# RWKV block times mixture of experts on one core: first expert product two tiles ahead, four result buffers, a ring of nine, 71 tiles, and a new order in the last round

## The reference

```python
s = rwkv(xn)            # ln0, ln1, time shift, k/v/r projections, a recurrence over 512 steps,
                        # output projection (Wo), ln2, channel mix: relu^2, Wfv, sigmoid gate (Wfr)
probs = softmax(xn @ Wg)                 # 8 experts, capacity T/8, each token ends at one expert
for e in range(8):
    h = gelu(xt @ W1[e]) @ W2[e]         # 256 -> 512 -> 256
    out = out + gate[:, None] * h
return x + s * silu(out)
```

## Time and profile before

| what | us |
|---|---|
| median of 3 executions | 1107.13 (1106.48 to 1108.46) |
| the profiled execution | 1109.16 |
| its span, first to last instruction | 1107.4 |
| TensorE busy | 1022.6 |
| VectorE busy | 899.7 |
| ScalarE busy | 689.0 |
| GpSimd busy | 386.0 |

### The profile page before, as it was taken

How to read it: one execution, slowest core, us unless ns; L and a number is a source line. 1 busy time by engine, 2 the same in 40 slices (tenths; PEclk the granted TensorE clock), 3 DMA queues, 4 the chain that set the end, 5 groups by cost and what they waited for, 6 DMA issues and landing times.

```text
span 1107.4 us, 19070 instructions
## 1 busy us (share of the span) xinstructions
PE 1022.6 (92%) x5440; PEld 838.0 (76%) x5440; DVE 899.7 (81%) x1996; ACT 689.0 (62%) x1233; POOL 386.0 (35%) x407
## 2 busy tenths in 40 slices
PE   4779999999999999999999699999897999999996
PEld 4457787777777767777676577777777999999996
DVE  5799888998988889888899979786554777887775
ACT  2638565676856758566585559567363665666664
POOL 3105314111101011010110065657804666666663
PEclk9879999999999999999999899999998999999998
DMA  8424230101101011010110011062602333333320
GB/s 290 166 76 134 77 114 19 39 4 55 57 0 57 0 57 57 0 57 0 57 38 20 10 49 58 1 190 79 221 31 78 104 110 103 110 111 104 100 71 16
DMA packets 60113, 80.79 MB, mean 73 GB/s; under 512 B 7806, under 2 KB 47359, under 8 KB 60034
## 3 DMA queue, kind: packets, MB, share of 16 engines
q1 hardware_dynamic: 48658, 54.69, 15.5%
q0 software_dynamic: 11392, 25.32, 7.6%
HBM read 65.17 MB, written 26.49 MB: 83 GB/s over the span
## 4 chain that ended last, share of the span: by engine, by line
PE 59%; DVE 19%; issue 7%; ACT 7%; POOL 6%; another core or an unknown queue 1%; DVEq 1%; DMA 1%; ACTq 0%; POOLq 0%
PE psKV L926 13%; PE psM L997 11%; PE psM L865 9%; PE psM L877 5%; POOL sorted_list L414 2%; DVE arena L1392 2%; PE psM L914 2%; DVE arena L1335 2%; PE psT L830 2%; ACT arena L619 2%; PE psR L786 2%; PE psM L895 2%; PE psR L1009 2%; DVE bnst L1314 2%; ACT arena L524 2%
## 5 line engine op out<-in xcount | busy, mean ns | idle before, releaser
L926 PE MATMUL psKV<-arena 128*128 128x256 f32 x1024 | 232.5, 381 | 4.1 <-ACT arena L619 4.1
L926 PEld LDWEIGHTS psKV<-arena 128*128 128x128 f32 x1024 | 192.9, 191 | 44.0 <-issue 17.7
L421 POOL TENSOR_SCALAR lnw<-mv 128x4 f32<-128x4 f32 x32 | 18.9, 592 | 509.5 <-DVE mv L1318 509.4
L997 PE MATMUL psM<-arena 128*128 128x128 f32 x1152 | 142.0, 277 | 0.0
L997 PEld LDWEIGHTS psM<-arena 128*128 128x128 f32 x1152 | 135.9, 194 | 0.1
L895 PE MATMUL psM<-mix_hi,wfk_hi 128*128 128x512 f32 x256 | 106.4, 416 | 21.8 <-ACT arena L615 21.6
L571 ACT ACTIVATE arena<-psM 128x512 f32<-128x512 f32 x64 | 36.5, 589 | 131.6 <-PE psM L865 131.6
L1335 DVE SCALAR_TENSOR_TENSOR arena<-arena,vecs 128x512 f32<-128x512 f32 x160 | 109.9, 746 | 0.0
L482 POOL DMA_INDIRECT out_dram<-arena,out_idx x72 | 83.9, 1165 | 73.9 <-DVE row_idx L1506 38.5
L524 ACT ACTIVATE arena<-s_ring,cf 128x256 f32 (+1 forms) x128 | 66.4, 591 | 58.9 <-POOL cf L426 58.7
L897 PE MATMUL psM<-mix_hi,wfk_lo 128*128 128x512 f32 x256 | 101.0, 394 | 0.0
(11 more groups left out here) (206 smaller groups left out, 2419.7 us busy)
## 6 DMA issues: line engine op xcount, KB each, us to landing
desk<-in_x SPq DMA_DIRECT2D x16, 512.0 KB, 4.8
arena<-in_x SPq DMA_DIRECT2D x16, 512.0 KB
desk<-in_xT SPq DMA_DIRECT2D x16, 512.0 KB, 4.3
xs_rows<-s_ring SPq DMA_DIRECT2D x16, 512.0 KB
xs_rows<-in_x SPq DMA_DIRECT2D x16, 512.0 KB
desk<-in_W SPq DMA_DIRECT2D x8, 512.0 KB
arena<-in_W SPq DMA_DIRECT2D x8, 512.0 KB
out_dram<-arena,out_idx POOLq DMA_INDIRECT x72
```

Source lines behind the costliest of these rows:

```text
L926: ins = pe.matmul(psKV[:, j // 2, (j % 2) * C:(j % 2 + 1) * C], kf2[:, h, j * P:(j + 1) * P], wfv[:, h, :], start=(h == 0), stop=(h == HC ...
L997: ins = pe.matmul(psM[:, i % 2, f * P:(f + 1) * P], w1_t[i % 2][:, k, f * P:(f + 1) * P], xnT[i % 2][:, k, :], start=(k == 0), stop=(k == ...
```

## The change

In the expert stage TensorE runs `mlp_in(t + 2)` ahead of `mlp_out(t)` instead of `mlp_in(t + 1)`, turns tile t + 4 instead of t + 3, and ScalarE follows (`gelu(t + 2)`, `take_xn(t + 4)`, `xn(t + 5)`). The hidden layer gets three buffers for each part, the result of the second product four places in PSUM (two of them where channel output was), the gate four, and the ring of row buffers grows from eight to nine. The loop runs over 71 tiles instead of 72. In the last round the output projection comes ahead of channel output on TensorE, GpSimd clears the rows behind the scale of ln2, and behind the last round ScalarE squares ahead of the sigmoid. VectorE's order in a step is the same.

```diff
-RING = 8
+RING = 9
+    TILES = NTILE + E - 1
@@
-        y_ps = [psM[:, 2, 0:C], psR[:, 0:C]]
+        y_ps = [psM[:, 2, 0:C], psR[:, 0:C], psKV[:, 0, 0:C], psKV[:, 1, 0:C]]
@@ gpsimd, round_
                 if not ahead:
                     add_to_list(b, 1)
+                rstd2(b)
+                if not ahead:
                     zero_rows()
-                rstd2(b)
@@ gpsimd, experts
-            for t in range(NT - RING):
+            for t in range(TILES):
                 scatter(t, t % RING)
-                gather(t + RING, t % RING)
-            for t in range(NT - RING, NT):
-                scatter(t, t % RING)
+                if t + RING < TILES:
+                    gather(t + RING, t % RING)
@@ scalar, behind the last round
+            squares(NB - 1, HC - 2, HC - 1)
             sigmoid_fr(NB - 1)
-            squares(NB - 1, HC - 2, HC - 1)
@@ scalar, experts
+            def gelu(t):
+                if t >= 3:
+                    act.wait_ge(S["y_done"], t - 2)
+                act.wait_ge(S["h_done"], t + 1)
+                act.activation(hT_t[t % 3], psM[:, t % 2, :], ACT.Gelu).then_inc(S["gelu_done"], 1)
+                act.activation(hT_hi[t % 3], psM[:, t % 2, :], ACT.Gelu).then_inc(S["h_hi_done"], 1)
@@ step(t)
-                    gelu(t + 1, (i + 1) % RING)
+                if t < TILES - 2:
+                    gelu(t + 2)
                 tanh(t, i)
-                    take_xn(t + 3, (i + 3) % RING)
-                    xn(t + 4, (i + 4) % RING, g + (i + 4) // RING)
+                if t < TILES - 4:
+                    take_xn(t + 4, (i + 4) % RING)
+                if t < TILES - 5:
+                    xn(t + 5, (i + 5) % RING, g + (i + 5) // RING)
@@ ahead of the steps
-            gelu(0, 0)
+            gelu(0)
             take_xn(2, 2)
+            gelu(1)
+            take_xn(3, 3)
+            xn(4, 4, 0)
@@ tensor, round_
-                if ffn:
+                if ffn and ahead:
                     channel_out(b - 1, 0)
                 project_out(b)
+                if ffn and not ahead:
+                    channel_out(b - 1, 0)
@@ tensor, mlp_out
                 wait_run(pe, S["h_lo_done"], t + 1)
-                if not (isinstance(t, int) and t < 2):
-                    wait_run(pe, S["combined"], t - 1)
+                if t >= 4:
+                    pe.wait_ge(S["combined"], t - 3)
+                elif t >= 2:
+                    pe.wait_ge(S["s_mult"], NB)
@@ tensor, step(t)
-                    mlp_in(t + 1, (i + 1) % RING)
+                if t < TILES - 2:
+                    mlp_in(t + 2, (i + 2) % RING)
                 mlp_out(t, i)
-                    turn_x(t + 3, (i + 3) % RING)
+                if t < TILES - 4:
+                    turn_x(t + 4, (i + 4) % RING)
@@ vector
             def split_h(t, i):
                 wait_run(v, S["h_hi_done"], t + 1)
-                v.tensor_tensor(hT_lo[i % 2], hT_t[i % 2], hT_hi[i % 2].bitcast(F32), ALU.subtract
+                v.tensor_tensor(hT_lo[t % 3], hT_t[t % 3], hT_hi[t % 3].bitcast(F32), ALU.subtract
```

More of the change, by code:

```diff
@@ L209, in ring @@
             return [arena[:, rc[0] - n * (d + 1):rc[0] - n * d] for d in range(depth)]
-        rows = ring(2 * C, RING)
+        rows = ring(2 * C, RING - 1)
         xn_t = ring(C, 2)
         xnT = [a.rearrange("p (k t) -> p k t", k=CH) for a in ring(C, 2)]
+        th_t = ring(C, 4)
         w1_t = [a.rearrange("p (k f) -> p k f", k=CH) for a in ring(CH * F, 2)]
[L215 to L220, removed]
+        hi_at = rc[0]
+        ring(F, 3)
+        rc[0] = max(rc[0], x_in_at)
+        rows += ring(2 * C, 1)
+        lo_at = rc[0]
+        hT_t = ring(F, 3)[::-1]
+        hT_h = same_place("hT_h", 3 * F, "arena", hi_at)
+        hT_l = same_place("hT_l", 3 * F, "arena", lo_at)
+        hT_hi = [hT_h[:, i * F:(i + 1) * F] for i in range(3)]
+        hT_lo = [hT_l[:, i * F:(i + 1) * F] for i in range(3)]
         out_t = ring(C, RING)
@@ L262, in rwkv_times_moe @@
         xs_store = xs_rows.rearrange("(n p) c -> p n c", p=P)
-        y_ps = [psM[:, 2, 0:C], psR[:, 0:C]]
+        y_ps = [psM[:, 2, 0:C], psR[:, 0:C], psKV[:, 0, 0:C], psKV[:, 1, 0:C]]
         def steps(eng, step, first=-3):
-            for t in range(first, NT):
+            for t in range(first, TILES):
                 step(t, t % RING, t // RING)
@@ L715, in xn @@
                 nf = info_t[i]
-                act.activation(xn_t[i % 2], rows[i][:, 0:C], ACT.Identity, scale=nf[:, 2:3], bias=nf[:, 3:4]
+                act.activation(xn_t[t % 2], rows[i][:, 0:C], ACT.Identity, scale=nf[:, 2:3], bias=nf[:, 3:4]
                                ).then_inc(S["xn_done"], 1)
@@ L985, in turn_x @@
                 for k in range(CH):
[L986 removed]
+                    ins = pe.transpose(psT[:, t % 2, k * P:(k + 1) * P], xn_t[t % 2][:, k * P:(k + 1) * P], ident)
                 ins.then_inc(S["turned"], 1)
@@ L996, in mlp_in @@
                     for k in range(CH):
-                        ins = pe.matmul(psM[:, i % 2, f * P:(f + 1) * P], w1_t[i % 2][:, k, f * P:(f + 1) * P],
-                                        xnT[i % 2][:, k, :], start=(k == 0), stop=(k == CH - 1))
+                        ins = pe.matmul(psM[:, t % 2, f * P:(f + 1) * P], w1_t[t % 2][:, k, f * P:(f + 1) * P],
+                                        xnT[t % 2][:, k, :], start=(k == 0), stop=(k == CH - 1))
                 ins.then_inc(S["h_done"], 1)
@@ L1003, in mlp_out @@
                 w = pe.value_load(src, min_val=0, max_val=(E - 1) * FK * C)
+                if t == 0:
+                    pe.wait_ge(S["w2_split"], 1)
                 wait_run(pe, S["h_lo_done"], t + 1)
[L1005 to L1006 removed]
+                if t >= 4:
+                    pe.wait_ge(S["combined"], t - 3)
+                elif t >= 2:
+                    pe.wait_ge(S["s_mult"], NB)
                 for f in range(FK):
                     n = slice(f * P, (f + 1) * P)
[L1009 to L1011 removed]
+                    pe.matmul(y_ps[t % 4], hT_hi[t % 3][:, n], w2_hi[:, ds(w + f * C, C)], start=(f == 0), stop=False)
+                    pe.matmul(y_ps[t % 4], hT_hi[t % 3][:, n], w2_lo[:, ds(w + f * C, C)], start=False, stop=False)
+                    ins = pe.matmul(y_ps[t % 4], hT_lo[t % 3][:, n], w2_hi[:, ds(w + f * C, C)],
                                     start=False, stop=(f == FK - 1))
```

37 lines of the change are left out of this document (14 added, 23 removed).

## The result

| | median us (lowest to highest, runs) |
|---|---|
| before, beside it | 1107.32 (1102.67 to 1112.06, 20) |
| after | 1100.82 (1097.74 to 1108.68, 20) |
| ratio | 0.9944, interval 0.9930 to 0.9958 |

The change is faster by 0.56%, some 6 us. The forecast was 1117 us and slower. The profiled execution has a span of 1098.7 us against 1107.4, that is -8.7. A "stop" is a stretch in which ScalarE stands idle although the input of its next instruction is ready.

The account below looks back on a forecast made before the run. TensorE was taken as the bound, with time lost at the expert stage's start. -4.6 - 1.7 + 0.2 + 14.9 - 0.8 + 2.0 = +10.0 us on 1109.16, for the median 1117; own forecast 1107 to 1125, range 1094 to 1130.

Parts of the forecast that it names:

- last round, squares, transposes: Ahead of the expert stage: earlier projection and scale -4.6 us, squares ahead of the sigmoid -1.7, one more transpose +0.2.
- start, X to M(4): Expert stage from tile 0's first product (X) to second product 4's last matmul (M(4)): +2 us.
- M(4) to the third tile from the end, less a step: Steady expert stage: 64 steps of 3.535 us plus 18.4 of late tiles, 244.6 against 229.7 us: +14.9.
- last two tiles: End of the expert stage: both first products long done, so the last two tiles take 4.7 instead of 5.5 us: -0.8.
- The chain of the copy: Steady stage: last matmul through tanh, out_idx and VectorE's W1 copy to the first product; 3.535 us a tile, not 3.42.
- the first case: Start of the expert stage if ScalarE didn't stop: second product 4 ends at 22.0 us instead of 28.8, -6.8.
- the second case: Start of the expert stage if ScalarE stops as before: second product 4 ends at 32.9 us, +4.1.
- The step that failed: Steady stage: the W1 copy's chain starts at tanh(t), so late tanhs reach TensorE in full, 18.4 us together.
- 13 late tiles: Steady stage of the kernel before: tiles late by over 0.75 us, not inherited; together 20.3 us, 18.4 after deductions.
- the lead pays: Rival, first product two tiles ahead: stops vanish or are covered, only W1 copy binds; loop -3.5, 1090 to 1103; 0.24.
- the rival had two or three falls: Rival, steady loop: TensorE's clock falls after longer waits, 5 us a fall; two or three give 1124 to 1134; 0.10.
- The sentence cited from the Trainium skill: Instruction blocks are prefetched, so crossing one is mostly hidden; not relied on, by it the sum would be 18.4 us less.

Follow-up runs that it names:

- e12: The kernel before, unchanged, run again for its trace on a chip without stops; 1091.05 us, a single execution.
- e1: The kernel before with only the three edits of the last round, expert stage as before; 1083.82 us, ratio 0.9943.
- e13: The changed kernel, nothing else altered, timed on a chip without stops; 1088.02 us, ratio 0.9972 to the kernel before.
- e5: The changed kernel, nothing else altered, timed again with its trace on a chip with stops; 1101.30 us, ratio 0.9948.
- e8: The changed kernel with made stops (four extra ScalarE copies, about 2.8 us) ahead of 12 gelus, chip with stops; 1130.20 us, ratio 1.0221.
- group 3: Third of five sets of follow-up runs, on a chip without stops; the kernel before beside it takes 1091.29 us.
- groups 1, 3, 4 and 5: The sets of follow-up runs on chips without stops; the kernel before beside them takes 1090.80, 1091.29, 1090.67 and 1090.89 us.
- e3: The changed kernel with the last round of the kernel before, so only the expert stage differs from before; 1094.88 us, ratio 1.0040.
- group 2: Second of five sets of follow-up runs, on a chip with stops; the kernel before beside it takes 1107.11 us.
- the first comparison: The changed kernel against the kernel before, ahead of the follow-up runs, chip not known; 1100.82 against 1107.32 us, ratio 0.9944.
- e14: The kernel before with the last round's edits and 71 tiles, first product not two tiles ahead, chip without stops; 1082.45 us, ratio 0.9924.
- e6: The kernel before with the last round's edits and 71 tiles, first product not two tiles ahead, chip with stops; 1096.92 us, ratio 0.9903.

## Why the prediction was wrong

By its own steps, on the profiled execution:

| step | forecast | measured |
|---|---|---|
| last round, squares, transposes | -6.1 | -9.6 (X 834.42 to 824.81) |
| start, X to M(4) | +2.0 | +2.6 (28.8 to 31.4) |
| M(4) to the third tile from the end, less a step | +14.9 | -0.8 (229.7 to 229.0) |
| last two tiles | -0.8 | -0.9 (5.5 to 4.6) |
| sum | +10.0 | -8.7 |

- **The last round was right.** Of the -9.6, 3.15 are there before it: receptance (L924, L914 before) starts at 772.64 against 775.79, behind rounds that did not change, and e12, the same program as before, starts it at 773.10, so they are not the change's. The 6.45 left are the 6.1 of the forecast, and e1 measured 6.2 by itself.
- **The chain of the copy was right**, 3.50 us for 3.535, and it binds nearly every tile.
- **The start came near by luck.** The +2.0 was a point between two cases. Without stops the start is 22.0 us (e13), as the first case had it; with them it is 31.4, 34.1 and 31.5 (the changed kernel, e5, e8), and the second case's 32.9 lies among these, but with other stops: 2.9, 2.5, 4.6 and 1.8 us ahead of gelu(3), tanh(1), gelu(4) and tanh(2) in the changed kernel, where I had 5.0 and 5.4 ahead of the first two.
- **The step that failed**: "The chain starts at tanh(t), so a late tanh now goes to TensorE in full", with 13 late tiles carried over for 18.4 us. Its first half holds (12 made stops: 28.9 us for 28, with the reserve above; the one natural stop, ahead of gelu(61): 4.0 us, clock included). The second does not: of the 18.4 us, 5.0 came (229.0 - 64 x 3.50; 2.8 over the 64 x 3.535 of the forecast), four of them from that one stop. I took waits that nothing in the trace explained as a constant of the program. They are none: the same program traced in group 3 (e12) has no stop, nor has any of the other thirteen traces of groups 1, 3, 4 and 5, and where there are stops the changed order of ScalarE's list had one in three traces. Why the order or its pace keeps them away stays open.
- This is the rival "the lead pays" (0.24): copy binds, stops away. Its price, 1090 to 1103, held the time. Its name was wrong: the lead doesn't pay, it costs 4 to 7 us, and it was the tile and the last round that paid. Had I priced the lead as it is without stops (+7, from e3), the forecast would have been -6.1 - 3.4 + 7 = -2.5 us, the -2.7 that e13 measured on a chip without them; with the 4.4 of group 2 it is -5.1, near the -5.8 of e5 and the -6.5 of the first comparison.
- The clock fell in the steady stage once (0.65 behind a wait of 1.71 us), where the rival had two or three falls.
- The sentence cited from the Trainium skill (Runtime: NRT & Kernel Launch, Instruction fetch mechanics), that crossing a block of instructions is "mostly hidden", would have given 18.4 us less, -8.4 on the profiled execution, where -8.7 came. On the chips without stops the traces agree with it: ScalarE has no stop in the stage. Whether the stops elsewhere have to do with the loading of instructions no run here shows.

## What to carry to other kernels

Before you add lookahead to a pipeline, follow every operand of the step that is moved: three of its four inputs got a tile more here, and the fourth, a copy queued behind the combine on VectorE, got one less and set the pace. A wait that the trace can't explain is not a term of a sum: price the change with it and without it, and see whether the sign hangs on it. And take a bundle apart; here two small edits gave 8 to 10 us (e14, e6) and the large one took back 4 to 7.

## What was not expected of the hardware

- The same program took 1107 us in two of the six comparisons and 1091 in the other four, on three chips (20 and 14 runs; 19, 13, 21 and 13). Between the two traces of it (1109.16 and 1091.05) lie 18.1 us, and 16.2 of them are in the expert stage (264.0 us from X to the last M, and 247.8), where ScalarE stops in one and not in the other.
- The stops have a rhythm but no fixed place. In the kernel before they stand ahead of gelu(31), (35), (39), (43), (47), (51) and (55), four tiles (20 of ScalarE's instructions) apart, in turn 2.0 and 2.8 us of idle time; in e6, whose ScalarE list in the stage is the same but for the tile less, ahead of gelu(41), (45), (49) and (53). Only gelu(31) is in both. (The expectation of e12 counts tiles from 1.)
- Instruction packets arrive throughout the stage; DMA queues of the changed kernel, 850 to 1060 us (packets, MB, share of 16 engines):
```profile
q0 software_dynamic: 7467, 21.32, 34.1%
q8 instruction: 17, 0.28, 0.5%
q14 instruction: 12, 0.10, 0.2%
```
  The kernel before has 16 and 12 such packets there, and 17 and 12 on the chip without stops (e12). So their number does not tell the two apart. Nor do their times: in the kernel before the last packet of q8 ends about 0, 4.2 and 6.5 us ahead of gelu(35), gelu(43) and gelu(51). What the stops are is open.
